# The tail of a Perceiver block on one core: a new order for the last tiles of the second output projection, a new Sinkhorn schedule with its scratch in PSUM, and VectorE mixing 24 units

## The chip, the cores and the metric

One core of a Trainium2 chip. The metric is the device time of one execution in microseconds. Before the change it is 1153.63 us, the median of three runs (1153.41 to 1156.05).

## The reference, cut to what matters

Three sublayers, each added to x, which has 8 x 64 tokens of 1024 numbers in float32: a cross attention with 32 heads, a self attention with 32 heads (its output projection is the last large product of the kernel), and a mixing block. Only the end of the second and the third matter here:

```python
x = x + attention2(layernorm(x))                 # ... @ Wo.T, with causal mask
# third sublayer, on h = layernorm(x) of this x:
x_norm = h * rsqrt(mean(h * h) + eps)
L      = x_norm @ [W_res; W_pre; W_post].T + base          # 16 + 4 + 4 numbers a token
H_res  = sinkhorn_log(L[16] as 4x4, 50 iterations, tau 0.1) # rows and columns in turn
H_pre, H_post = softmax(L[4]), softmax(L[4])
H_res  = (1 - g) * I + g * H_res                             # g = sigmoid(gate)
y      = (sum_n H_pre[n] * h[n]) @ W_branch                  # h as 4 streams of 256
out    = x + (H_res @ h_streams + H_post x y)
```

A Sinkhorn iteration here works on K = exp(logits / tau), shifted: it makes the row sums of K * v, inverts them to u, makes the column sums of K * u, inverts them to v.

## The kernel before, in words

The kernel is written by hand in five programs, one for each engine, tied by semaphores; nothing is reordered by a planner, so the order of the text is the order of the work. Tokens are four tiles (t = 0 to 3) of 128 rows. PSUM has eight banks of 512 numbers (`ps[:, k, :]`). Weights are transposed by VectorE (L1373), and split in a high part (ScalarE, L967) and a low part (VectorE, L1381); a tile of 512 output columns takes 24 matmuls (L864): eight chunks of the contraction, three products each.

**The last products.** The loop `for b in range(16)` (L885, TensorE) does the second attention's query units 21 and 22 (b = 0 to 7) and its output projection as units 23 (columns 0 to 511, b = 8 to 11, tiles 0 to 3) and 24 (columns 512 to 1023, b = 12 to 15, tiles 0 to 3). The attention itself is woven in up to b = 10: transposed queries (L733), scores (L750), transposed probabilities (L765), weighing (L780), transposed outputs (L790). On VectorE the loop L1789 serves the same steps: in step b it adds the product of step b - 1 to x (`add_tile`, L1663) with half of its statistics (L1784), reads scores (L1730), scales outputs (L1744, L1750), centres (L1736, L1738), transposes weight chunks (`turns`), makes their low parts (`later`: of unit 24 chunks 0, 1 in step 9, 2 to 4 in step 10, 5 to 7 in step 11) and the low part of an output (L1759), on which the second half of the next L765 waits.

When the second half of a tile's row is added (`last_stats3`, L1812), VectorE ends its statistics and GpSimd takes two roots (L2036). TensorE transposes the finished rows (`turn_rows`, L801), ScalarE copies them out (L1259), TensorE makes the 24 logits (`logits`, L810, 16 records a tile), and VectorE reads them (L1830, L1833). W_branch and the three small matrices arrive by DMA (L443, L445) and are transposed at L917; L923 multiplies them by a matrix of ones.

**The Sinkhorn chains.** The four tiles are two chains of VectorE instructions: chain 0 for tiles 0 and 1, chain 1 for tiles 2 and 3. An iteration is six small instructions, each waiting for the one before it in its chain:

```python
            def iterate(chains, fresh=None, last=None):        # L1916
                ... tk = Kx * v        (L1921)   ... ua = row sums of tk   (L1927)
                ... ua = 1 / ua        (L1930)   ... tk = Kx * ua          (L1903)
                ... v  = column sums   (L1906)   ... v  = 1 / v            (L1910)
```

With both chains given, the instructions of the two alternate. All operands lie in the SBUF tile `small`. Chain 0 does its first iteration and HEAD = 4 more alone (L1977 to L1980), then the logits of tile 3 are read (L1981), chain 1 is set up and does its first iteration, and 20 iterations are done jointly. Then the epoch: each chain's sums go through a logarithm on ScalarE (`log_chain`), are added to the logits (`recentre`, L1940) and exponentiated anew, while the other chain does 4 iterations alone; then 21 joint iterations, `finish(0)` (L1951 to L1956), 4 iterations of chain 1 alone and `finish(1)`. From the start of chain 1's first iteration to the end of its last that is 20 + 4 + 4 + 21 + 4 = 53 turns. VectorE's queue is in order, so nothing of it overlaps anything else of VectorE.

**Branch and mixing.** ScalarE and TensorE make the branch y of each tile (L1289, L822, L829) and its base x + H_post * y (L839, L843); tiles 0 and 1 stay open in banks (0, 1) and (2, 3), tiles 2 and 3 go through banks (4, 5) back to SBUF (L1302). The final mixing has 64 units of 128x256 (tile, output stream i, input stream j). For tiles 0 and 1 ScalarE makes 32 diagonal matrices when chain 0 is finished (L1336), TensorE multiplies (L853, two records a product) and ScalarE copies out (L1341). For tiles 2 and 3 VectorE does 32 instructions after chain 1 (L2023): tile 2 with all four streams at once, tile 3 in two halves. SyncE stores in five DMAs (L446 to L450), in the order tile 0, tile 2, tile 1, tile 3 first half, tile 3 second half, each waiting for its part.

Of the kernel before, what the change touches and what calls it, by code (L numbers as in the profile page):

```python
# [25 lines left out]
P = 128  # L26
# [11 lines left out]
ITERS, EPOCH, HEAD = 50, 25, 4  # L38
# [10 lines left out]
def perceiver(nc, x, ctx_in, mask_x, wq1, wk1, wv1, wo1, qn_w, kn_w, wq2, wk2, wv2, wo2,  # L49
# [10 lines left out]
    with es:  # L60
# [76 lines left out]
        tk = cols(64)  # L137
        uv = cols(32)
        luv = cols(32)
# [154 lines left out]
        def _(sp):  # L294
# [156 lines left out]
            sp.wait_ge(out_stored, 16 * 5)  # L451
# [3 lines left out]
        def _(pe):  # L455
# [337 lines left out]
            def turn_rows(t, half):  # L793

                pe.wait_ge(acc_free, (57 if half else 53) + t)
                if t == 0:
                    pe.wait_ge(o2_lo, 8)
                else:
                    pe.wait_ge(f_ready, 2 * t - 1 + half)
# [5 lines left out]
            def logits(t):  # L805
                pe.wait_ge(f_ready, 2 * t + 2)
                if t >= 2:
                    pe.wait_ge(lg_read, t - 1)
                for c in range(NC):
                    mm = pe.matmul(lg[t % 2], xT[t % 2][:, c, :], w24T[:, c, :], start=(c == 0), stop=(c == NC - 1))  # L810
                mm.then_inc(lg_done, 1)
# [20 lines left out]
            def base(t):  # L832

                pe.wait_ge(lg_read, 4)
                if t == 3:
                    pe.wait_ge(base_added, 1)
                for half in range(2):
                    bank = ps[:, base_banks[t][half], :]
# [3 lines left out]
                    for i in (2 * half, 2 * half + 1):  # L842
                        mm = pe.matmul(bank[:, (i % 2) * CW:(i % 2 + 1) * CW], dmix[t % 2][:, 4 + i, :], yb,  # L843
                                       start=False, stop=(t >= 2 and i % 2 == 1))
                mm.then_inc(base_done, 1)

            def mix(t):
                for half in range(2):
                    bank = ps[:, base_banks[t][half], :]
                    for i in (2 * half, 2 * half + 1):  # L850
                        for j in range(NSTR):
                            pe.wait_ge(d_res, 16 * t + 4 * i + j + 1)
                            mm = pe.matmul(bank[:, (i % 2) * CW:(i % 2 + 1) * CW], dres[t][:, 4 * i + j, :],  # L853
# [31 lines left out]
            for b in range(16):  # L885
                n, t = 21 + b // NT, b % NT
                pe.wait_ge(acc_free, 43 + b)
# [3 lines left out]
                def at_11():  # L891
                    if b == 0:
                        turn_key(2)
                    elif b <= 8:
                        turn_query(b - 1)
                    elif b >= 12:
                        if b >= 13:
                            turn_rows(b - 13, 1)
                        turn_rows(b - 12, 0)

                def at_17():
                    if 3 <= b <= 10:
                        turn_out2(b - 3)
                tile_products(n, t, at_11, at_17)
# [8 lines left out]
                if b == 11:  # L913
# [5 lines left out]
                if b == 12:  # L919
# [5 lines left out]
                if b >= 13:  # L925
                    logits(b - 13)
            turn_rows(3, 1)
            logits(3)
# [3 lines left out]
            for t in range(2):  # L932
                mix(t)
# [24 lines left out]
        def _(sc):  # L958
# [296 lines left out]
            def copy_rows(t, half):  # L1255
                sc.wait_ge(f_done, 2 * t + half + 1)
# [10 lines left out]
            asked = [0, 0]  # L1267

            def answer(c, dst, src, func):

                asked[c] += 1
                sc.wait_ge(sk_in[c], asked[c])
                sc.activation(dst, src, func).then_inc(sk_out[c], 1)
# [4 lines left out]
            def log_chain(c):  # L1278
                answer(c, luv.rearrange("p (s c n) -> p c s n", s=2, c=2)[:, c],
                       uv.rearrange("p (s c n) -> p c s n", s=2, c=2)[:, c], ACT.Ln)  # L1280

            def branch(t):
# [16 lines left out]
                if t >= 2:  # L1299
                    sc.wait_ge(base_done, t + 1)  # L1300
                    for half in range(2):
                        a = sc.activation(xr[:, t, half * UW:(half + 1) * UW], ps[:, base_banks[t][half], :], ACT.Copy)  # L1302
                    a.then_inc(base_added, 1)

            copy_rows(0, 0)
            sc.wait_ge(s24_done, 1)
            sc.activation(s24, ps[:, 3, 192:216], ACT.Copy).then_inc(s24_ready, 1)
            copy_rows(0, 1)
            copy_rows(1, 0)
            normalise_out(0)  # L1310
            copy_rows(1, 1)
            copy_rows(2, 0)
            normalise_out(1)
            copy_rows(2, 1)
            copy_rows(3, 0)
            exp_chain(0)
            exp_chain(0)
            copy_rows(3, 1)
            normalise_out(2)
            exp_chain(1)  # L1320
# [4 lines left out]
            branch(0)  # L1325
            branch(1)
            log_chain(0)
            exp_chain(0)
            log_chain(1)
            exp_chain(1)  # L1330
            branch(2)
            branch(3)
            for t in range(2):
                sc.wait_ge(h_ready, 1)
                for n in range(16):
                    sc.activation(dres[t][:, n, :], ident[:], ACT.Copy, scale=hres[:, 16 * t + n:16 * t + n + 1]  # L1336
# [805 lines left out]
```

## Time and profile before

| what | value |
|---|---|
| median of 3 runs | 1153.63 us |
| the profiled execution, its own time | 1153.41 us |
| its span, first to last instruction | 1151.6 us |
| TensorE matmul busy | 1071.5 us (93%) |
| VectorE busy | 808.7 us (70%) |
| ScalarE busy | 477.0 us (41%) |
| granted TensorE clock over the span | 0.978 |

Busy shares are means over the whole span. Starts in the trace's views are microseconds from the span's start. In a timeline a row is one or more instructions of one line in a row: start, time from the first's start to the last's end, engine, line, operation, operands and count; in brackets the idle time before it and what ended it.

### The profile page before, as it was taken

The page shows a single profiled execution, that of the slowest core. Times are in us where ns is not written, and L with a number is a line of the kernel's source. Part 1 is how long each engine was busy: PE and PEld are TensorE (multiplying, and loading weights), DVE is VectorE, ACT ScalarE, POOL GpSimd, SP SyncE. Part 2 cuts the span into 40 slices and gives each one's busy share as a digit, 9 for nine tenths or more (in the row PEclk, how much of TensorE's full clock was granted, in tenths as well). Part 3 has the DMA queues.
Part 4 walks back from the last instruction along what each step waited for, and adds up shares of the span by engine and source line. Part 5 has one row for each costly group of instructions (what it writes and reads, how often), then busy time and mean ns, then how long its engine had stood idle before and what let it go on. Part 6 is the DMA issues. An engine that isn't in the chain of part 4 may idle for free.

```text
span 1151.6 us, 17668 instructions
## 1 busy us (share of the span) xinstructions
PE 1071.5 (93%) x6392; PEld 899.6 (78%) x6392; DVE 808.7 (70%) x1843; ACT 477.0 (41%) x989; POOL 154.7 (13%) x162
## 2 busy tenths in 40 slices
PE   5999999999999999999999999999999999895565
PEld 3888888888888887888888887888888778784444
DVE  6744447567768868776678876675547799836998
ACT  4523324354454446544544455432223334313334
POOL 0000000333223222332332220000001000000000
PEclk9999999999999999999999999999999999997778
DMA  9876757243443233344334312899835322000001
GB/s 236 189 163 144 159 124 168 55 101 89 102 105 73 68 73 69 75 98 101 93 90 104 70 33 61 172 218 245 172 74 109 57 42 35 14 2 1 0 1 73
DMA packets 163803, 111.12 MB, mean 96 GB/s; under 512 B 73224, under 2 KB 155784, under 8 KB 163744
## 3 DMA queue, kind: packets, MB, share of 16 engines
q1 hardware_dynamic: 161488, 109.24, 43.3%
q10 hardware_dynamic: 2256, 1.11, 0.4%
q8 instruction: 35, 0.57, 0.2%
q14 instruction: 24, 0.20, 0.1%
HBM read 90.91 MB, written 18.87 MB: 95 GB/s over the span
## 4 chain that ended last, share of the span: by engine, by line
PE 82%; DVE 14%; ACT 2%; issue 1%; DMA 1%; POOL 0%; ACTq 0%; DVEq 0%
PE ps L533 29%; PE ps L476 28%; PE ps L864 8%; PE ps L462 5%; PE ps L544 4%; PE ps L561 4%; DVE wt L1381 1%; DVE xr L2023 1%; DVE small L1906 1%; DVE small L1930 1%; DVE small L1910 1%; DVE small L1903 1%; DVE small L1927 1%; DVE small L1921 1%; PE ps L650 1%
## 5 line engine op out<-in xcount | busy, mean ns | idle before, releaser
L533 PE MATMUL ps<-wt,act 128*128 128x512 f32 x1536 | 389.1, 396 | 0.0
L476 PE MATMUL ps<-wt,act 128*128 128x512 f32 x1440 | 330.1, 391 | 4.0 <-DVE wt L1381 3.9
L476 PEld LDWEIGHTS ps<-wt,act 128*128 128x128 f32 x1440 | 271.1, 189 | 60.8 <-DVE act L1365 4.3
L533 PEld LDWEIGHTS ps<-wt,act 128*128 128x128 f32 x1536 | 275.9, 188 | 49.5
L1381 DVE TENSOR_TENSOR wt<-raw,wt 128x512 fp32r<-128x512 f32 x192 | 120.0, 682 | 84.9 <-ACT wt L967 84.9
L967 ACT ACTIVATE wt<-raw 128x512 fp32r<-128x512 f32 x192 | 106.5, 623 | 94.5 <-PE ps L476 52.7
L1365 DVE TENSOR_TENSOR act<-ps,act 128x512 fp32r<-128x512 f32 x112 | 75.9, 683 | 78.4 <-ACT act L962 78.4
L1373 DVE STREAM_TRANSPOSE raw<-raw 128x1024 f32<-128x1024 f32 x92 | 108.0, 1217 | 31.4 <-DMA raw<-in_L_xattn_o_proj_w 20.7
L864 PE MATMUL ps<-wt,act 128*128 128x512 f32 x480 | 121.0, 400 | 1.7 <-issue 1.0
L962 ACT ACTIVATE act<-ps 128x512 fp32r<-128x512 f32 x112 | 65.9, 596 | 114.2 <-PE ps L462 113.9
L2036 POOL TENSOR_TENSOR small<-small 128x4 f32<-128x4 f32 (+2 forms) x64 | 70.8, 1109 | 278.5 <-DVE small L1395 213.7
L864 PEld LDWEIGHTS ps<-wt,act 128*128 128x128 f32 x480 | 87.0, 188 | 19.8 <-issue 1.7
L1047 ACT ACTIVATE G<-G,small 128x256 f32<-128x256 f32 x128 | 64.1, 502 | 80.7 <-DVE small L1492 80.7
L2063 POOL TENSOR_TENSOR act<-xr,act 128x1024 fp32r<-128x1024 f32 x30 | 71.9, 2396 | 110.2 <-ACT act L1000 110.2
L462 PE MATMUL ps<-ident,G 128*128 128x128 f32 x448 | 67.4, 276 | 16.2 <-ACT G L973 10.3
L462 PEld LDWEIGHTS ps<-ident,G 128*128 128x128 f32 x448 | 54.5, 141 | 30.6 <-issue 9.9
L544 PE MATMUL ps<-act 128*128 128x256 f32 x384 | 60.0, 292 | 0.6 <-DVE act L1365 0.6
L1012 ACT ACTIVATE G<-ps 128x512 f32<-128x512 f32 x32 | 19.1, 598 | 97.3 <-PE ps L476 97.3
L1488 DVE SCALAR_TENSOR_TENSOR G<-ps,small,G 128x256 f32<-128x256 f32 x128 | 55.4, 474 | 5.7 <-PE ps L544 5.7
L561 PEld LDWEIGHTS ps<-act 128*128 128x128 f32 x384 | 54.4, 189 | 5.5 <-DVE act L1365 0.4
L2054 POOL TENSOR_TENSOR small<-small 128x4 f32<-128x4 f32 x32 | 6.5, 202 | 374.6 <-DVE small L1509 374.6
L561 PE MATMUL ps<-act 128*128 128x256 f32 x384 | 56.2, 282 | 0.0
(145 smaller groups left out, 1086.4 us busy)
## 6 DMA issues: line engine op xcount, KB each, us to landing
xr<-in_ctx SPq DMA_DIRECT2D x64, 256.0 KB, 5.7
raw<-in_L_xattn_o_proj_w SPq DMA_DIRECT2D x32, 512.0 KB, 13.9
raw<-in_L_xattn_q_proj_w SPq DMA_DIRECT2D x28, 512.0 KB, 9.6
q_rows<-G SPq DMA_DIRECT2D x64, 128.0 KB, 3.5
xr<-q_rows SPq DMA_DIRECT2D x16, 512.0 KB
ot_hi<-spare SPq DMA_DIRECT2D x64, 128.0 KB, 2.6
act<-ot_hi SPq DMA_DIRECT2D x32, 256.0 KB, 9.0
raw<-in_L_xattn_k_proj_w SPq DMA_DIRECT2D x8, 512.0 KB, 9.0
```

What stands on the lines that cost most here:

```text
L462: tr = pe.transpose(bank[par][:, j * P:(j + 1) * P], src, ident[:])
L476: mm = pe.matmul(banks[t], lhs(p == 2, c, t), wt[:, n_slot, int(p == 1), c, :], start=(acc_from and q == 0), stop=(acc_to and q == 3 * NC ...
L533: mm = pe.matmul(bank, src[int(p == 2)][:, c, kt * P:(kt + 1) * P], wt[:, slot, int(p == 1), c, :], start=(q == 0), stop=(q == 3 * NC - 1))
L544: mm = pe.matmul(sacc[:, j * 256:(j + 1) * 256], lhs[p], kT[r][:, g, :], start=(p == 0 and r == 0), stop=(p == 1))
L561: mm = pe.matmul(oacc, vN[r][:, kt, g * P:(g + 1) * P], pT[p][:, kt * 256:(kt + 1) * 256], start=(n == 0), stop=(n == 5))
L864: mm = pe.matmul(acc2[t], act[:, int(n >= 23), int(p == 2), k:k + P], wt[:, n % 2, int(p == 1), c, :], start=(q == 0), stop=(q == 3 * NC - 1))
L967: sc.activation(blocks16(wt_dst(par, 0, c)), raw_chunks(par, c) if slot is None else raw_chunks(slot, c), ACT.Copy).then_inc(w_hi, 1)
L1365: v.tensor_tensor(dst, four(bank[par]) if shaped else bank[par], hi_.bitcast(F32), ALU.subtract).then_inc(lo_done, 1)
L1373: v.transpose(y, y).then_inc(w_turned, 1)
L1381: v.tensor_tensor(blocks16(wt_dst(par, 1, c)), raw_chunks(slot, c), blocks16(wt_dst(par, 0, c)).bitcast(F32), ALU.subtract).then_inc(w_lo, 1)
L2036: pool.tensor_tensor(dst, src, mhalf[:, 0:n], ALU.pow).then_inc(signals, 1)
L2063: pool.tensor_tensor(ctx_dst(ctxT, 1, kt), ctx_src(kt), ctx_dst(ctxT, 0, kt).bitcast(F32), ALU.subtract).then_inc(ctx_lo, 1)
```

## The change

1. Order of the output projection: a hand-written order of tile and half replaces "all first halves, then all second halves". Steps b = 8 to 15 now do (tile, half) = (0,0), (1,0), (0,1), (1,1), (2,0), (3,0), (2,1), (3,1). Unit 24 is thus first used in step 10 in place of step 12, so its low parts are made in steps 9 (chunks 0 to 3) and 10 (chunks 4 to 7). The half statistics of tiles 0 and 1 move behind the low part of step 10.
2. The transposes of rows and the logits follow the new order; the logits of tile 2 and the first half of those of tile 3 are computed inside step 15, ahead of its last six matmuls.
3. Chain 0 starts after the logits of tile 1 and does 1 + 3 + 3 + 1 iterations (`LEAD`) between the last additions. The reading of tile 3's logits comes after the last of these.
4. The epoch needs no logarithm: ScalarE gives exp of half the centred logits once (`answer(c, A, 0.5)`), and in iteration 25 the scaled matrix becomes the new Kx by `fold_outer` (in place of the column scaling) and two multiplications by that root (`fold_root`, twice). Chains stay joint through it. After chain 1's first iteration there are 41 joint ones, one with the finish of chain 0 woven in, and 7 of chain 1 alone: 49 turns.
5. `tk` (scaled matrix) and the row sums `us` are in PSUM bank 5; `Kx` and the column sums `vs` stay in SBUF.
6. Mixing: the first half of tile 2 goes to TensorE (bank 4, 8 more diagonals and 8 more products, after those of tile 1), the rest of tiles 2 and 3 stays with VectorE as 16 + 8 instructions. Bases that go back to SBUF use the upper halves of banks 6 and 7. There are six stores, the first half of tile 2 third in order.

```diff
-ITERS, EPOCH, HEAD = 50, 25, 4
+ITERS, EPOCH = 50, 25
+LEAD = (1, 3, 3, 1)
+LAST = ((0, 0), (1, 0), (0, 1), (1, 1), (2, 0), (3, 0), (2, 1), (3, 1))
...
+        tk, us = ps[:, 5, 0:64], ps[:, 5, 64:80]
...
-        base_banks = [(0, 1), (2, 3), (4, 5), (4, 5)]
+        open_banks = [(ps[:, 0, :], ps[:, 1, :]), (ps[:, 2, :], ps[:, 3, :]), (ps[:, 4, :],)]
+        late_base = ps[:, 6:8, 256:512]
...
-            for t, half, signal, count in ((0, None, mix_out, 2), (2, None, out_ready, 1), (1, None, mix_out, 4),
-                                           (3, 0, out_ready, 2), (3, 1, out_ready, 3)):
+            for t, half, signal, count in ((0, None, mix_out, 2), (1, None, mix_out, 4), (2, 0, mix_out, 5),
+                                           (2, 1, out_ready, 1), (3, 0, out_ready, 2), (3, 1, out_ready, 3)):
...
             for b in range(16):
                 n, t = 21 + b // NT, b % NT
+                if b >= 8:
+                    t, n = LAST[b - 8][0], 23 + LAST[b - 8][1]
...
-                    elif b >= 12:
-                        if b >= 13:
-                            turn_rows(b - 13, 1)
-                        turn_rows(b - 12, 0)
+                    elif b == 11:
+                        turn_rows(0, 0)
+                        turn_rows(0, 1)
+                    elif b == 12:
+                        logits(0)
+                        turn_rows(1, 0)
+                        turn_rows(1, 1)
+                    elif b == 13:
+                        turn_rows(2, 0)
+                    elif b == 14:
+                        turn_rows(3, 0)
+                    elif b == 15:
+                        turn_rows(2, 1)
...
+                    if b == 15:
+                        logits(2)
+                        logits(3, 0, 4)
...
             turn_rows(3, 1)
-            logits(3)
+            logits(3, 4, NC)
             for t in range(NT):
                 branch(t)
                 base(t)
-            for t in range(2):
+            for t in range(3):
                 mix(t)
...
-                     6: (23, (4, 5)), 7: (23, (6, 7)), 9: (24, (0, 1)), 10: (24, (2, 3, 4)), 11: (24, (5, 6, 7))}
+                     6: (23, (4, 5)), 7: (23, (6, 7)), 9: (24, (0, 1, 2, 3)), 10: (24, (4, 5, 6, 7))}
...
             def exp_chain(c):
-                answer(c, Kx[:, 32 * c:32 * c + 32], A[:, 32 * c:32 * c + 32], ACT.Exp)
+                sc.wait_ge(sk_in[c], 1)
+                answer(c, Kx)
+                sc.wait_ge(sk_in[c], 2)
+                answer(c, Kx)
+                sc.wait_ge(sk_out[c], 2)
+                answer(c, A, 0.5)
...
+            diagonals(0)
+            diagonals(1)
+            mixed(0, 0)
+            mixed(0, 1)
+            mixed(1, 0)
+            diagonals(2)
+            mixed(1, 1)
+            mixed(2, 0)
...
-            ua = [uv[:, 8 * c:8 * c + 8] for c in range(2)]
-            ub = [uv[:, 16 + 8 * c:24 + 8 * c] for c in range(2)]
+            ua = [us[:, 8 * c:8 * c + 8] for c in range(2)]
+            ub = [vs[:, 8 * c:8 * c + 8] for c in range(2)]
...
+            def iterate(chains):
+
+                fold = [c for c in chains if iterated[c] == EPOCH]
                 for c in chains:
+                    iterated[c] += 1
+                    if c in fold:
+                        fold_outer(c)
+                    else:
+                        scale_cols(c)
+                for c in fold:
+                    fold_root(c, tk)
+                    fold_root(c, Kx)
...
-            last_stats3(0)
-            last_stats3(1)
+            add_last(1, 1)
             logits(0)
-            last_stats3(2)
+            add_last(2, 0)
             logits(1)
             centre_rows(0)
             centre_cols(0)
-            last_stats3(3)
             first_iteration3(0)
+            for _ in range(LEAD[0]):
+                iterate((0,))
+            add_last(3, 0)
+            for _ in range(LEAD[1]):
+                iterate((0,))
+            add_last(2, 1)
+            for _ in range(LEAD[2]):
+                iterate((0,))
             logits(2)
-            for _ in range(HEAD):
+            add_last(3, 1)
+            for _ in range(LEAD[3]):
                 iterate((0,))
             logits(3)
             centre_rows(1)
+            centre_cols(1)
...
             first_iteration3(1)
-            joint = EPOCH - 1 - HEAD
-            for k in range(joint):
-                iterate((0, 1), last=0 if k == joint - 1 else None)
+            for k in range(ITERS - iterated[0]):
+                iterate((0, 1))
...
+            v.wait_ge(base_added, 3)
+            mix(((2, 1), (3, 0)))
+            mix(((3, 1),))
```

## Rows read from the trace of the kernel before

**Rows 1.** The chain that ended last, its shares of the span by engine.
```profile
PE 82%; DVE 14%; ACT 2%; issue 1%; DMA 1%; POOL 0%; ACTq 0%; DVEq 0%
```
**Rows 2.** Busy time by stretch: length, PE, PEld, DVE, ACT, POOL, clock, DMA share, GB/s.
```profile
1062.50:1098.70 36.20, 15.29 (x64) 11.78 (x64) 34.59 (x268) 14.66 (x36) 0.00 (x0) 0.69 0.00 1
...
1128.60:1134.90 6.30, 5.75 (x20) 4.88 (x21) 5.37 (x29) 6.21 (x22) 0.00 (x0) 0.72 0.00 0
1134.90:1145.40 10.50, 9.79 (x46) 8.28 (x44) 10.15 (x24) 5.40 (x16) 0.00 (x0) 1.00 0.25 100
```
**Rows 3.** Timeline of VectorE between the last product and chain 1's first iteration.
```profile
1047.92 0.69 DVE L1663 TENSOR_TENSOR xr<-ps,xr 128x512 f32<-128x512 f32 x1 [1.28 <-PE ps L864]
...
1049.81 0.18 DVE L1903 TENSOR_TENSOR small<-small 128x32 f32<-128x32 f32 x1
...
1056.21 0.20 DVE L1830 SCALAR_TENSOR_TENSOR G<-G,small,ps 128x24 f32<-128x24 f32 x1
...
1058.76 0.19 DVE L1903 TENSOR_TENSOR small<-small 128x32 f32<-128x32 f32 x1 [0.30 <-ACT small L1273]
```
**Rows 4.** Timeline of VectorE, first instruction of successive iterations: joint, then alone.
```profile
1069.57 0.31 DVE L1921 TENSOR_TENSOR small<-small 128x32 f32<-128x32 f32 x2
...
1070.96 0.30 DVE L1921 TENSOR_TENSOR small<-small 128x32 f32<-128x32 f32 x2
...
1131.34 0.19 DVE L1921 TENSOR_TENSOR small<-small 128x32 f32<-128x32 f32 x1
...
1132.73 0.19 DVE L1921 TENSOR_TENSOR small<-small 128x32 f32<-128x32 f32 x1
```
**Rows 5.** Matmul records of the logits of one tile, in the chain.
```profile
1039.70 1.70 PE ps L810 x16
```
**Rows 6.** Timeline around steps 9 and 10 of the loop, VectorE and TensorE.
```profile
1001.38 0.68 DVE L1759 TENSOR_TENSOR act<-ps,act 128x512 fp32r<-128x512 f32 x1
...
1002.12 0.65 PE L765 MATMUL ps<-ident,raw 128*128 128x128 f32 x4 [1.21 <-DVE act L1759]
...
1004.53 4.40 PE L864 MATMUL ps<-wt,act 128*128 128x512 f32 x18
...
1005.70 1.89 DVE L1381 TENSOR_TENSOR wt<-raw,wt 128x512 fp32r<-128x512 f32 x3
```
**Rows 7.** Timeline of the mixing on ScalarE and TensorE.
```profile
1128.69 9.45 ACT L1336 ACTIVATE raw<-ident,small 128x128 f32<-128x128 f32 x32 [7.04 <-DVE small L1956]
...
1129.15 15.55 PE L853 MATMUL ps<-G,raw 128*128 128x256 f32 x64 [8.61 <-ACT raw L1336]
```
**Rows 8.** The chain's mixing on VectorE, in order of time, and the last stores.
```profile
1134.89 1.69 DVE xr L2023 x4
...
1141.82 0.89 DVE xr L2023 x2
...
1145.56 0.89 DVE xr L2023 x2
...
out<-xr SPq DMA_DIRECT2D x2, 256.0 KB, 2.5
```
**Rows 9.** VectorE's groups by form (busy us, mean ns), without and with a PSUM operand.
```profile
L1921 DVE TENSOR_TENSOR small<-small 128x32 f32<-128x32 f32 x96 | 15.4, 191 | 0.4
...
L1930 DVE RECIPROCAL small<-small 128x8 f32<-128x8 f32 x98 | 16.3, 200 | 0.6
...
L1744 DVE RECIPROCAL small<-ps 128x16 f32<-128x16 f32 x8 | 2.0, 249 | 3.1 <-PE ps L780 3.1
...
L1833 DVE SCALAR_TENSOR_TENSOR small<-G,small 128x24 f32<-128x24 f32 x4 | 1.0, 244 | 0.1
L1830 DVE SCALAR_TENSOR_TENSOR G<-G,small,ps 128x24 f32<-128x24 f32 x4 | 0.9, 213 | 0.0
```
**Rows 10.** Timeline of VectorE: two independent instructions that read PSUM, one behind the other.
```profile
889.90 0.28 DVE L1699 TENSOR_TENSOR spare<-ps,G 128x128 f32<-128x128 f32 x1
890.10 0.28 DVE L1700 TENSOR_TENSOR spare<-ps,G 128x128 f32<-128x128 f32 x1
```

More of the change, by code:

```diff
@@ L803, in turn_rows, with logits @@
                 tr.then_inc(f_done, 1)
-            def logits(t):
-                pe.wait_ge(f_ready, 2 * t + 2)
-                if t >= 2:
+            def logits(t, c0=0, c1=NC):
+                pe.wait_ge(f_ready, max(TURNED[t, h][0] for h in range(c0 // 4, (c1 + 3) // 4)))
+                if c0 == 0 and t >= 2:
                     pe.wait_ge(lg_read, t - 1)
-                for c in range(NC):
+                for c in range(c0, c1):
                     mm = pe.matmul(lg[t % 2], xT[t % 2][:, c, :], w24T[:, c, :], start=(c == 0), stop=(c == NC - 1))
-                mm.then_inc(lg_done, 1)
+                if c1 == NC:
+                    mm.then_inc(lg_done, 1)
             def branch(t):
@@ L834, in base @@
                 pe.wait_ge(lg_read, 4)
[L835 to L838, printed above, removed]
+                for half in range((2, 2, 1, 0)[t]):
+                    bank = open_banks[t][half]
                     pe.matmul(bank, ident[:], xr[:, t, half * UW:(half + 1) * UW], start=True, stop=False)
@@ L1255, in copy_rows @@
             def copy_rows(t, half):
-                sc.wait_ge(f_done, 2 * t + half + 1)
+                sc.wait_ge(f_done, TURNED[t, half][0])
                 if half == 0 and t >= 2:
@@ new lines, in invert_rows, with scale_rows, sum_cols, invert_cols @@
+            def invert_rows(c):
+                stepped(c)
+                step(c, v.reciprocal(ua[c], ua[c]))
+            def scale_rows(c):
+                stepped(c)
+                step(c, v.tensor_tensor(rows3(of(tk, c)), rows3(of(Kx, c)), over_j(ua[c]), ALU.mult))
+            def sum_cols(c):
+                stepped(c)
+                step(c, v.tensor_reduce(two(ub[c]), cols4(of(tk, c)), AX, ALU.add))
+            def invert_cols(c):
+                stepped(c)
+                step(c, v.reciprocal(ub[c], ub[c]))
@@ new lines, in first_iteration3, with fold_outer, fold_root @@
+            def first_iteration3(c):
+                answered(c, 2)
+                scale_rows(c)
+                sum_cols(c)
+                invert_cols(c)
+            def fold_outer(c):
+                stepped(c)
+                rows = two(ua[c]).unsqueeze(3).broadcast_to([P, 2, NSTR, NSTR])
+                step(c, v.tensor_tensor(rows4(of(tk, c)), rows, over_i(ub[c]), ALU.mult))
+            def fold_root(c, dst):
+                answered(c, 3)
+                stepped(c)
+                step(c, v.tensor_tensor(of(dst, c), of(tk, c), of(A, c), ALU.mult))
@@ L1999, in _, with mix @@
                     done(v.tensor_tensor(h8r, h8r, h8m.unsqueeze(2).broadcast_to([P, 8, NSTR]), ALU.mult), mix_ready)
-            for k in range(HEAD):
-                if k == HEAD // 2:
-                    recentre(0)
-                iterate((1,), last=1 if k == HEAD - 1 else None)
-            for k in range(HEAD):
-                if k == HEAD // 2:
-                    recentre(1)
-                iterate((0,), fresh=0 if k == 0 else None)
-            for k in range(ITERS - EPOCH - HEAD):
-                iterate((0, 1), fresh=1 if k == 0 else None)
-            finish(0)
-            for k in range(HEAD):
+            iterated[1] += 1
+            finish_cols(0)
+            scale_cols(1)
+            finish_gate(0)
+            sum_rows(1, tk)
+            finish_diagonal(0)
+            invert_rows(1)
+            scale_rows(1)
+            sum_cols(1)
+            invert_cols(1)
+            for _ in range(ITERS - iterated[1]):
                 iterate((1,))
-            finish(1)
+            finish_cols(1)
+            finish_gate(1)
+            finish_diagonal(1)
             settle()
-            for t, parts in ((2, ((0, 1, 2, 3),)), (3, ((0, 1), (2, 3)))):
-                v.wait_ge(base_added, t - 1)
-                for streams in parts:
-                    for j in range(NSTR):
-                        settle()
-                        for i in streams:
+            def mix(pieces):
+                for j in range(NSTR):
+                    settle()
+                    for t, half in pieces:
+                        for i in (2 * half, 2 * half + 1):
                             c = 16 * t + 4 * i + j
```

231 lines of the change are left out of this document (107 added, 124 removed).

## The prediction

> **What bounds the kernel now.** I read the chain that ended last first. TensorE has 82% of it and VectorE 14% [rows 1]: products carry the kernel until the last tile at 1047.92 us [rows 3], and from there VectorE carries nearly all of the last 104 us. The table by stretch confirms it: from 1062.5 to 1098.7 VectorE is busy 34.59 of 36.20 us, TensorE 15.29, ScalarE 14.66 [rows 2]. So a saving outside VectorE's queue in the tail is worth nothing, and one inside it is worth its full length unless ScalarE, TensorE or the stores end later.
>
> In the tail there are four pieces: from the last product to chain 1's first iteration (1047.92 to 1058.76, rows 3), 53 turns of the chains, the finish, and VectorE's mixing from 1134.89 [rows 8]. A joint iteration takes 1.39 us (1069.57 to 1070.96) and one of a chain alone takes the same 1.39 (1131.34 to 1132.73) [rows 4]. That is six steps of 0.232 us: the length is the wait of an instruction for its predecessor, and the second chain rides for nothing. It rides nearly at the limit, though. Two instructions of L1921 together last 0.31, one lasts 0.19 [rows 4, 9], so the second starts 0.12 after the first, half a step. Shorter waits can help a joint turn only a little, unless an instruction also occupies the engine for less.
>
> **The change, part by part.** Times are against the profiled execution (span 1151.6, own time 1153.41, 0.2 under the median).
>
> *Unit 24 two steps earlier.* Step 9 now makes four low parts in place of two, ahead of L1759, and the second half of L765 waits for that (it was idle 1.21 us for it already) [rows 6]. Three low parts last 1.89 us, so two are 1.25 us: TensorE is later by +1.2. The statistics that leave step 9 (0.7) don't pay for it, as VectorE then waits for the products of L780 anyway. In step 10 the product starts at 1004.53 + 1.2 = 1005.8 and wants chunk 4 after 12 matmuls at 0.24 us (18 last 4.40), 1008.7; VectorE makes it from about 1006.9, after scaling the outputs, to 1007.6, and chunk 7 to 1009.5 against 1010.7 or later. Covered, by about 1 us at the tightest. The small matrices' transposes move to the end of step 10, about 1012; their DMAs are issued once the last weighing is done, 1005.9, and a store of the largest one's 256 KB takes 2.5 us [rows 8], so they are there by 1010.
>
> *Logits inside step 15.* One tile's logits and half of another's come ahead of the last matmuls: 1.70 + 0.85 = +2.55 us [rows 5]. The transposes move but stay the same number before the last product's end (8 halves less one). So the last product ends at 1047.9 + 1.2 + 2.55 = 1051.7.
>
> *Chain 0's lead.* Its 1 + 3 + 3 iterations (9.7 us) must fit between additions. Chain 0 is set up after step 12, which I place at 1031; its first iteration and one more end at about 1035.6, the product of step 13 at 1037.4. A further three take 4.2 us of the 6.2 us of step 14 (5.5 us of products and 0.6 of transposes), beside 1.4 of addition and statistics; the same again in step 15 with 1.9. They fit by 0.5 us in step 14 and more in step 15, so they cost nothing. If they did not fit, TensorE's next transpose would wait for the addition queued behind them, at most 1.4 us.
>
> *Chain 1's start.* Behind the last product stand the addition and last statistics, 1.89 us (1047.92 to 1049.81), one iteration, 1.39, then the logits: 1051.7 + 3.3 = 1055.0 in place of 1056.21 [rows 3]. TensorE's last transposes, the copy and half of the logits need about 3.2 us in the same time, a near tie. From there to the first iteration is the same work, 2.55 us. Gain: -1.2.
>
> *The turns.* 49 in place of 53: 4 x 1.39 = -5.6. Two recentrings at 0.2 go (-0.4), the steps that a fresh matrix spared come back (+0.2), the finish of chain 0, 0.6 us alone, is woven into a turn (-0.6). The two folds add two dependent steps each: 4 x 0.232 = +0.9, and here the other chain waits. Together -5.4; I take -5.2, since the woven finish has some longer instructions. The logarithms go from ScalarE, which was not on the path.
>
> *Mixing.* Half a tile leaves VectorE. A half lasts 1145.56 - 1141.82 = 3.7 us [rows 8]; the remaining 16 go four to a step as tile 2 did (6.9 us for 16) and the last 8 as a half. -3.7.
>
> *The other side of the mixing.* Let T be the finish of chain 0. ScalarE's 32 diagonals take 9.45 and TensorE's 32 products 15.6 us from 0.45 after it [rows 7], to T + 16.1. The eight further diagonals can start after the third copy, T + 13.4, and are done at T + 15.8; eight products at 0.43 (46 records in the 9.8 to 10.1 us after 1134.9 [rows 2]) end at T + 19.5, their copy at T + 20.2. VectorE: T + 11.4 (0.9 for the rest of the woven turn, 7 x 1.39, finish 0.75) + 6.9 + 3.7 = T + 22.0. TensorE's side has 1.8 us to spare. But SyncE waits in order, so three stores of 256 KB start at T + 20.2 to 21 and share the engines with the last, where before the last had them alone (2.5 us [rows 8]): +0.5.
>
> *PSUM.* The operands of five of six steps change: four write PSUM, four read it. No VectorE instruction before writes PSUM. Reads: 24 columns take 213 ns with a PSUM operand and 244 without [rows 9]; 128 columns take 281 ns with PSUM [rows 10] against 191 for 32 without [rows 9], 0.94 ns for each further column, so nothing is left for PSUM; the reciprocal of 16 numbers from PSUM takes 249, that of 8 from SBUF 200, a difference that the numbers or the memory may make. Occupancy: two independent PSUM readers of 128 columns start 0.20 apart [rows 10]; without 128 x 0.94 ns that leaves 0.08, and a chain's pair leaves 0.12 - 0.03 = 0.09. So reading PSUM is as quick as SBUF or some 10 ns quicker. Bounds for a touched instruction: -31 ns (244 to 213) and +49 (the reciprocals, all of it put on PSUM); for the writes I keep the same two, having nothing nearer. I take -10 ns for each of the four reading steps and nothing for the writes: 0.04 a turn, x 49 = 2.0, of which the occupancy limit may keep back some: -1.7.
>
> The Trainium skill says the opposite ("VectorE: DVE Perf Modes", section "The TRN2 errata"): a fixed 58 cycles at 0.96 GHz for SBUF sources and 120 for PSUM sources, an estimated 65 ns more per instruction. By it the sum would end near 1167, above the time before. For reads the rows here disagree with it; for writes no row shows either.
>
> Sum: -1.2 - 5.2 - 3.7 + 0.5 - 1.7 = -11.3; 1153.4 - 11.3 = 1142.1 us.
>
> **The rivals.**
> *A, PSUM is dearer (slower).* If each touched instruction occupies VectorE for d more, a joint turn pays eight of them, since the engine is nearly full, and a turn alone four: 41 x 8 + 8 x 4 = 360 d, against the 9.6 us gained without PSUM. Break-even is d = 27 ns; at the upper bound, 49 ns, it is +17.6, 1161 us; at 10 to 20 ns, 1147 to 1151. Against it stand the reads [rows 9, 10]; for it, that no write was seen and that the two reciprocals differ. Chance 0.15: 0.04 still faster, 0.04 level, 0.07 slower. The skill's page of above is a rule for this side.
> *B, the lead stalls TensorE.* Unit 24 or the lead comes late in steps 10 to 15 by 2 to 4 us: 1145 to 1148, faster all the same. Room of 0.9 and 0.5 us speaks both ways. Chance 0.08.
> *C, TensorE's mixing becomes the end.* The granted clock was 0.72 as the mixing began after a gap and 1.00 later [rows 2]; branches now end earlier, so the gap is longer. If the first half of the 40 products went at 1.2 GHz, some 0.4 us more each, that is +8 less the spare 1.8: about 1148. Before, it rose after some 3 us. Chance 0.05.
> *D, PSUM is quicker than I take.* Occupancy falls by 12 ns per touched instruction: 360 x 0.012 = 4.3, 1139.5; at twice that 1135. Chance 0.2.
> *E, the chains don't gain,* because a joint turn of one fold blocks both and the order of semaphores costs what the four turns gave: 1148 to 1152. The steps are all in the trace already, so 0.02.
>
> **How the numbers follow.** Forecast 1142.1, between 1139.5 and 1146, has 0.5. The range is 1135 to 1150: it takes in B, C, D and the cheap end of A. What the measurement can tell from no change is 0.3%, 3.5 us. Faster by more (under 1150.2): 0.5 + D 0.2 + B 0.08 + C 0.05 + A 0.04 = 0.87; same: A 0.04 + E 0.02 = 0.06; slower: A 0.07.
>
> **What would show it.** In the new trace: the last product's addition at 1051 to 1052; chain 1's first iteration near 1057.5; a joint turn of 1.33 to 1.39 us (above 1.45 is A, under 1.30 is D); 24 mixing instructions in 10.6 us; the last copy on ScalarE 1 to 2 us ahead of VectorE's end. It is wrong if a turn departs by over 0.1 us, or if the last addition is past 1054.

## The result and the profile after

The median of four runs is 1146.84 us (1146.20 to 1147.55), against 1154.84 us (1153.41 to 1156.87) for four runs of the kernel before on the same chip: ratio 0.9934, interval 0.9919 to 0.9948, so faster. The profiled execution took 1146.2 us with a span of 1144.4 (before 1153.41 and 1151.6): the span is 7.2 us shorter, where the working asked for 11.3; by the medians it is 8.0. Direction and range held, but about a third of the expected gain is missing, and the time lies just above the 1139.5 to 1146 us to which the forecast gave even chances.

The chain that ended last, shares of the span by engine [answers to rows 1]:

```profile
PE 81%; DVE 14%; DMA 2%; ACT 2%; issue 1%; ACTq 0%; POOL 0%; DVEq 0%; SPq 0%
```

The shares hardly moved, so they can't say where the gain went. VectorE's timeline can (start, time, engine, line, operation, operands, count, idle time before and what ended it) [rows 3, 4, 8]:

```profile
1044.02 0.69 DVE L1700 TENSOR_TENSOR xr<-ps,xr 128x512 f32<-128x512 f32 x1 [0.41 <-PE ps L884]
...
1052.66 0.69 DVE L1700 TENSOR_TENSOR xr<-ps,xr 128x512 f32<-128x512 f32 x1 [1.86 <-PE ps L884]
...
1058.13 0.19 DVE L1954 TENSOR_TENSOR ps<-small,ps 128x32 f32<-128x32 f32 x1
...
1058.71 0.32 DVE L1942 TENSOR_TENSOR ps<-small 128x32 f32<-128x32 f32 x2
...
1060.12 0.32 DVE L1942 TENSOR_TENSOR ps<-small 128x32 f32<-128x32 f32 x2
...
1130.57 10.53 DVE L2092 SCALAR_TENSOR_TENSOR xr<-G,small,xr 128x256 f32<-128x256 f32 x24
```

Cut at the same milestones, the two spans differ so:

| from, to | before | after | difference | forecast |
|---|---|---|---|---|
| start, last addition | 1047.92 | 1052.66 | | |
| start, chain 1's first iteration | 1058.76 | 1058.13 | -0.6 | -1.2 |
| to VectorE's mixing (the turns) | 76.13 | 72.43 | -3.7 | -6.9 (turns -5.2, PSUM -1.7) |
| VectorE's mixing | 14.30 | 10.53 | -3.8 | -3.7 |
| to the end of the span | 2.41 | 3.30 | +0.9 | +0.5 |

Four turns went, yet a joint turn lasts 1.41 us (1058.71 to 1060.12) where it took 1.39 [rows 4]. By form, between 1060 and 1120 us (busy us, mean ns of one) [rows 9]:

```profile
L1950 DVE RECIPROCAL ps<-ps 128x8 f32<-128x8 f32 x81 | 13.4, 210 | 0.0
L1962 DVE RECIPROCAL small<-small 128x8 f32<-128x8 f32 x83 | 13.0, 196 | 0.0
L1942 DVE TENSOR_TENSOR ps<-small 128x32 f32<-128x32 f32 x80 | 12.6, 198 | 0.0
L1954 DVE TENSOR_TENSOR ps<-small,ps 128x32 f32<-128x32 f32 x81 | 12.5, 194 | 0.0
L1946 DVE TENSOR_REDUCE ps<-ps 128x8 f32<-128x32 f32 x79 | 12.5, 198 | 0.0
L1958 DVE TENSOR_REDUCE small<-ps 128x8 f32<-128x32 f32 x81 | 12.3, 189 | 0.0
```

The reciprocal that reads and writes PSUM takes 210 ns where the one in SBUF [rows 9] takes 200. TensorE around steps 9 and 10 [rows 6], and the busy time by stretch (columns of rows 2):

```profile
1001.43 0.60 PE L769 MATMUL ps<-ident,raw 128*128 128x128 f32 x4
1002.96 0.66 PE L769 MATMUL ps<-ident,raw 128*128 128x128 f32 x4 [0.93 <-DVE act L1796]
1004.30 1.74 PE L784 MATMUL ps<-G,raw 64*64 64x33 f32 x64 [0.69 <-ACT raw L1255]
1005.97 5.32 PE L884 MATMUL ps<-wt,act 128*128 128x512 f32 x18
```

```profile
1004.00:1012.00 8.00, 7.70 (x88) 6.57 (x89) 3.42 (x7) 2.57 (x6) 0.00 (x0) 0.79 0.18 48
```

The 18 matmuls that lasted 4.40 us [rows 6] last 5.32, and the granted clock of the stretch is 0.79 where it had been 1.00: part of it ran at 1.2 GHz in place of 2.4.

### The profile page after: what moved, and what is told of

Its sections match the earlier page's. It is cut to its first block, busy times and chain, and to the rows that moved or that the text cites. A ratio compares the mean times of both kernels' runs of the same rounds, so it can differ in the third digit from the quotient of the medians.

```text
span 1144.4 us, 17715 instructions
## 1 busy us (share of the span) xinstructions
PE 1076.0 (94%) x6414; PEld 903.8 (79%) x6414; DVE 807.2 (71%) x1837; ACT 475.1 (42%) x991; POOL 155.6 (14%) x162
## 4 chain that ended last, share of the span: by engine, by line
PE 81%; DVE 14%; DMA 2%; ACT 2%; issue 1%; ACTq 0%; POOL 0%; DVEq 0%; SPq 0%
PE ps L480 28%; PE ps L537 27%; PE ps L884 8%; PE ps L466 5%; PE ps L548 3%; PE ps L565 3%; DVE wt L1418 2%; DMA xr<-q_rows 1%; DVE ps L1950 1%; DVE small L1962 1%; DVE ps L1954 1%; DVE ps L1946 1%; DVE small L1958 1%; DVE ps L1942 1%; PE ps L654 1%
```

## The experiments

Four questions: what PSUM does to a turn, what the wait in step 9 does to TensorE, what the order of the stores costs, and what chain 0's lead buys. Every experiment is the changed kernel with the edit shown. They ran on three chips: each ratio is against the kernel before on the same chip, and medians of different chips are compared only roughly.

**All scratch in SBUF.**

```diff
-        vs = cols(16)
-        tk, us = ps[:, 5, 0:64], ps[:, 5, 64:80]
+        vs, us, tk = cols(16), cols(16), cols(64)
```

> The changed kernel with the scaled matrix and the row sums in SBUF again, as before; all else as changed. Theory P (the PSUM operands make a turn longer): a turn goes from 1.41 us to the 1.39 of before, alone and joint; over 49 turns the mixing on VectorE starts 1.1 to 1.3 us earlier after chain 1's first iteration (71.2 us in place of 72.4), and the span ends near 1143.2. Theory Q (the longer turn comes from TensorE and ScalarE being busier beside the chains, or from the new order of instructions): a turn stays at 1.41 and the span at 1144.4. The forecast's own view (PSUM quicker by 10 ns a reading step): a turn gets longer, 1.45.

Ratio 0.9932 (0.9919 to 0.9944), median 1145.41 us, by time no different from the change. Its groups by form in the same stretch:

```profile
L1961 DVE RECIPROCAL small<-small 128x8 f32<-128x8 f32 x83 | 13.3, 201 | 0.0
L1957 DVE TENSOR_REDUCE small<-small 128x8 f32<-128x32 f32 x83 | 13.3, 200 | 0.0
L1949 DVE RECIPROCAL small<-small 128x8 f32<-128x8 f32 x83 | 13.2, 200 | 0.0
L1953 DVE TENSOR_TENSOR small<-small 128x32 f32<-128x32 f32 x83 | 12.7, 191 | 0.0
L1941 DVE TENSOR_TENSOR small<-small 128x32 f32<-128x32 f32 x81 | 12.6, 191 | 0.0
L1945 DVE TENSOR_REDUCE small<-small 128x8 f32<-128x32 f32 x83 | 12.5, 186 | 0.0
```

The turns go back to 1.39 us and their stretch to 71.28 (1059.56 to 1130.84), 1.15 shorter: that is PSUM's share. TensorE at work beside the chains is not what makes PSUM dear: from 1100.7 to 1118 us, where it is idle in the changed kernel, the reciprocal on PSUM takes 217 ns and the other five forms 190 to 200, against 207 and 188 to 198 while it works (1064 to 1100). The span did not shrink, since in this execution the clock between 1004 and 1012 was 0.57 and the last addition came at 1054.12, 1.5 later. A single profiled span doesn't show one microsecond of the chains; their own stretch does, and it is what I compare below. It repeats well: 72.43 to 72.45 us in all seven executions with the change's scratch.

**One operand at a time.** Only the matrix `tk`, only the sums `us`, or only the matrix scaled by rows, in a buffer of its own:

```diff
# matrix only
-        vs = cols(16)
-        tk, us = ps[:, 5, 0:64], ps[:, 5, 64:80]
+        vs, us = cols(16), cols(16)
+        tk = ps[:, 5, 0:64]
# sums only
+        vs, tk = cols(16), cols(64)
+        us = ps[:, 5, 64:80]
# rows-scaled matrix only; tr is also what sum_cols and finish_cols read
+        vs, us, tk = cols(16), cols(16), cols(64)
+        tr = ps[:, 5, 0:64]
-step(c, v.tensor_tensor(rows3(of(tk, c)), rows3(of(Kx, c)), over_j(ua[c]), ALU.mult))
+step(c, v.tensor_tensor(rows3(of(tr, c)), rows3(of(Kx, c)), over_j(ua[c]), ALU.mult))
```

> Only the scaled matrix in PSUM, the row sums in SBUF. Theory P, by the durations in the changed kernel against before (write of 32 numbers 201 against 193 ns, sum over columns read with a stride 191 against 202, reciprocal of the row sums 216 against 203): the reciprocal is back at 203, the sum over columns stays at 191, so a turn is 1.39 to 1.40. Theory Q: 1.41 as in the changed kernel.

> Only the row sums in PSUM, the scaled matrix in SBUF. Theory P: the reciprocal stays at 216 ns, the strided sum goes back to 202, the write of the matrix to 193: a turn of 1.41 to 1.42, the longest of the four. Theory Q: 1.41, the same as all the others.

> Only the matrix scaled by rows goes to PSUM, a buffer of its own, and is read from there by the strided sum over columns; the matrix scaled by columns, both kinds of sums and Kx are in SBUF. Theory P: the write costs 8 ns more and the strided read 11 less, so a turn is 1.385 to 1.39, not above the turn with all in SBUF. Theory Q: no difference among e1 to e4.

Each ran once: 1145.86, 1145.99 and 1144.93 us, too close to tell apart; the stretch of the turns tells them apart:

| scratch in PSUM | stretch of the turns | against all SBUF, per turn (of 49) |
|---|---|---|
| none | 71.28 | |
| matrix | 71.67 | +8 ns |
| sums | 71.95 | +14 ns |
| both (the change) | 72.43 | +23 ns |
| rows-scaled matrix alone | 71.01 | -6 ns |

The matrix alone, by form (1060 to 1120 us):

```profile
L1958 DVE TENSOR_REDUCE small<-ps 128x8 f32<-128x32 f32 x82 | 12.6, 190 | 0.1
L1946 DVE TENSOR_REDUCE small<-ps 128x8 f32<-128x32 f32 x80 | 12.3, 190 | 0.0
```

The upper line is the column sum, which reads across the rows of the matrix (200 with all in SBUF), the lower the row sum, which reads along them (186). The sums alone:

```profile
L1950 DVE RECIPROCAL ps<-ps 128x8 f32<-128x8 f32 x82 | 13.7, 212 | 0.0
L1946 DVE TENSOR_REDUCE ps<-small 128x8 f32<-128x32 f32 x82 | 12.7, 194 | 0.1
L1954 DVE TENSOR_TENSOR small<-small,ps 128x32 f32<-128x32 f32 x81 | 12.3, 186 | 0.0
```

So each use has its own price: writing PSUM costs 5 to 8 ns, the reciprocal on it 12, reading the matrix along its rows 4; the column sum gains 10 (190 against 200) and the multiplication by the inverted sums 5. The differences of the five forms with a PSUM operand add up to nearly what the turn does, since a step waits for the one before it: for the change +7 +12 +10 +3 -11 = +21 ns by form, +23 measured. The sixth form, the reciprocal in SBUF, was touched by no edit and still lies between 196 and 201 ns, so single differences of 5 ns and less are not sure. The version that keeps only the paying read in PSUM is the shortest of the five, by 0.27 us; two later kernels with this scratch show 71.02. The sums alone were expected to give the longest turn (1.41 to 1.42 us); it is the change itself that does.

**The wait in step 9.** The low part of the output, on which TensorE waits, goes ahead of the four low parts of unit 24:

```diff
+                if b == 9:
+                    lo_out2(b - 3)
                 if b in later:
                     for c in later[b][1]:
                         lo_unit(later[b][0], c)
-                if 3 <= b <= 10:
+                if 3 <= b <= 10 and b != 9:
                     lo_out2(b - 3)
```

> The changed kernel, but in step 9 VectorE makes the low part of the attention output (L1796) before the four low parts of unit 24, not behind them. Theory S (the four low parts ahead of it hold TensorE up, and the gap also lowers TensorE's granted clock in step 10, where the first 18 matmuls lasted 5.3 us against 4.4 before): the second half of the transposed probabilities starts near 1000.7 in place of 1003.0, the clock is 1.00 from 1004 to 1012, the last addition starts near 1049.5 in place of 1052.7, and the span is 1141 to 1142. Rival L (the last addition is late by the logits inside step 15 alone, and the clock dip is chance): the clock stays at 0.8 there, the last addition moves to 1051.5 at most and the span to 1143.

Ratio 0.9929 (0.9915 to 0.9943), median 1146.39 us: no more than the change, where a span of 1141 to 1142 us was expected. The wait is gone and the clock in step 10 is whole, but a stretch at 1.2 GHz came later. Its TensorE timeline:

```profile
1001.93 1.04 PE L769 MATMUL ps<-ident,raw 128*128 128x128 f32 x8
...
1004.77 4.38 PE L884 MATMUL ps<-wt,act 128*128 128x512 f32 x18
...
1046.24 2.75 PE L815 MATMUL ps<-G,raw 128*128 128x24 f32 x24
1048.84 2.53 PE L884 MATMUL ps<-wt,act 128*128 128x512 f32 x6
1052.15 1.12 PE L806 MATMUL ps<-ident,xr 128*128 128x128 f32 x4 [0.78 <-DVE xr L1700]
1053.95 1.90 PE L815 MATMUL ps<-G,raw 128*128 128x24 f32 x8 [0.69 <-ACT raw L1293]
```

The addition of step 14 comes 2.1 us earlier than in the changed kernel (1041.89 against 1044.02), but the last six matmuls take 2.53 us in place of 1.65, the last transposes 1.12 in place of 0.66 and the last logits 1.90 in place of 1.07. Chain 1's first iteration starts at 1058.17, where it was. The low clock was hardly chance of this one execution: the granted clock over the span was 0.976 to 0.979 in the five executions of this experiment, and 0.979 to 0.982 in the nine of the changed kernel.

**The order of the stores.** SyncE takes the late half of tile 2 and the first of tile 3, which VectorE finishes, ahead of the half that TensorE finishes:

```diff
-            for t, half, signal, count in ((0, None, mix_out, 2), (1, None, mix_out, 4), (2, 0, mix_out, 5),
-                                           (2, 1, out_ready, 1), (3, 0, out_ready, 2), (3, 1, out_ready, 3)):
+            for t, half, signal, count in ((0, None, mix_out, 2), (1, None, mix_out, 4), (2, 1, out_ready, 1),
+                                           (3, 0, out_ready, 2), (2, 0, mix_out, 5), (3, 1, out_ready, 3)):
```

> The changed kernel, but SyncE stores the second half of tile 2 and the first half of tile 3 before the first half of tile 2, which comes from TensorE. Theory T (the end hangs on TensorE's mixing through SyncE's order: three stores are issued only when ScalarE's last copy is done at 1139.9, and the last store 0.2 us late behind them): the two stores go out at 1137.5, the stretch from the end of VectorE's mixing to the end of the span goes from 3.3 to 2.5 us, the span to 1143.6. Rival: the last store takes its time anyway and the stretch stays at 3.0 or more.

Ratio 0.9917 (0.9901 to 0.9932), median 1145.12 us. From VectorE's end to the end of the span it is 2.45 us in place of 3.30. By the medians the gain over the change is 1.7 us, and the intervals overlap, so the time alone doesn't show it; the profiled span (1144.6) hides it, its last addition being at 1053.69. One profile would be thin, as this tail varies: in the nine executions with the old order and the full lead it is 2.87 to 4.05 us, 3.48 in the mean, and in the three with the new one 2.45 to 2.48.

**The first logits of tile 3 behind the last product.**

```diff
                     if b == 15:
                         logits(2)
-                        logits(3, 0, 4)
...
+            logits(3, 0, 4)
             turn_rows(3, 1)
             logits(3, 4, NC)
```

> The changed kernel, but the first half of the logits of tile 3 stands behind the last product of step 15, not ahead of its last six matmuls. By the trace the last product ends 0.85 us earlier and TensorE does the half while VectorE adds, so the last logits and chain 1's first iteration come 0.7 to 0.9 us earlier (1057.3 in place of 1058.1 at an equal start of step 15) and the span is 1143.6. If chain 1's start hangs on VectorE's queue (addition, statistics, one iteration) and not on TensorE, the gain is as large, since that queue starts with the last product too. Rival: the transposes of the last half wait behind the half of the logits and nothing is gained.

Ratio 0.9922 (0.9907 to 0.9937), median 1145.58 us. From the addition of step 14 to the last it is 7.74 us (1045.42 to 1053.16) in place of 8.64, and from there to chain 1's first iteration still 5.48: the eight records fit beside VectorE's last addition and cost nothing there. The wait of step 9 (2.51) and the low clock after it are as they were.

**Both of TensorE's edits together, and the change run again beside it.** The first joins the edits of step 9 and of the logits; the second is the changed kernel, unedited.

> The changed kernel with two edits together: the low part of the output first in step 9 (as e5) and the first half of tile 3's logits behind the last product (as e7). Theory C (each gap or thin stretch of TensorE is paid again in granted clock; e5 removed the one in step 10, but 24 thin matmul records in a row ahead of the last six products brought 1.2 GHz from 1049.3, e7 removed those but kept step 10's): with both gone the clock is 1.00 from 1004 to the last product, the last addition starts near 1048.5, 4 us before that of the changed kernel, and the time is 4 us under e10's. Rival A (the edits simply add): e5 and e7 gained 0 to 1 us each against the changed kernel, so 1 us or less under e10, and e8's gain came from the stores and the PSUM part.

> The changed kernel itself, unedited, on the same chip as its variants: 0.993 of the kernel before, 1144 to 1146 us beside 1153.5. Its last addition lies between 1052 and 1054 by how long TensorE runs at 1.2 GHz in steps 9 and 10. If that were chance of one execution, some profile would show 1051 as the sum of the forecast had it.

Ratios 0.9894 (0.9879 to 0.9910) and 0.9943 (0.9930 to 0.9957), medians 1141.08 and 1147.33: 6.2 us between them (5.6 by the ratios), where 4 were expected, and the intervals lie clear of each other. Each edit alone had stood 0.9 and 1.8 us under the change run again by the medians, on another chip, and 1.6 and 2.4 by the ratios, with intervals of some 1.7 us to either side that overlap that of the change. So the times show what the two give together, and not that it is more than their sum. TensorE's timeline of the changed kernel in this execution:

```profile
999.13 0.60 PE L769 MATMUL ps<-ident,raw 128*128 128x128 f32 x4
1002.24 0.66 PE L769 MATMUL ps<-ident,raw 128*128 128x128 f32 x4 [2.50 <-DVE act L1796]
1003.58 1.93 PE L784 MATMUL ps<-G,raw 64*64 64x33 f32 x64 [0.69 <-ACT raw L1255]
1005.44 6.36 PE L884 MATMUL ps<-wt,act 128*128 128x512 f32 x18
```

and of the joined edits:

```profile
999.21 1.35 PE L769 MATMUL ps<-ident,raw 128*128 128x128 f32 x8
1001.25 1.14 PE L784 MATMUL ps<-G,raw 64*64 64x33 f32 x64 [0.69 <-ACT raw L1255]
1002.31 4.40 PE L884 MATMUL ps<-wt,act 128*128 128x512 f32 x18
...
1043.80 1.86 PE L815 MATMUL ps<-G,raw 128*128 128x24 f32 x16
1045.50 1.65 PE L884 MATMUL ps<-wt,act 128*128 128x512 f32 x6
1046.99 0.97 PE L815 MATMUL ps<-G,raw 128*128 128x24 f32 x8
```

Both start level (999.1 and 999.2). The product of step 10 starts 3.1 us earlier without the wait: 2.5 for the wait and 0.8 for the weighing (1.14 against 1.93), less small things. It then lasts 1.96 us less. The logits give 0.9 more. That is 6.0, and the last addition is indeed at 1047.19 against 1053.17. So of the 5.1 us between the two up to the product's end nearly 2.8 (0.8 + 1.96) is granted clock that came after the wait. This is one pair of executions; the product alone varied by over 1 us where the wait stood (below).

**Everything that paid.** The rows-scaled matrix in PSUM, both of TensorE's edits and the order of the stores; and the same with the change's scratch.

> All together: low part of the output first in step 9, store order, half of the logits behind the product, and in the chains only the matrix scaled by rows in PSUM. If the parts add: 3.2 us from step 9, 0.8 from the logits, 0.8 from the stores and 1.4 from the turns, of which TensorE's mixing (its copy at 1139.9 in the changed kernel, VectorE's end at 1141.1) may keep back 0.5: a span near 1138.5, 0.5% under the changed kernel. If TensorE's mixing sets the end, the turns' part is lost and it is 1139.5 to 1140.

> e8 with the chains' scratch back in PSUM as the change has it (scaled matrix and row sums). Theory P: a turn is 1.416 us against 1.386 in e8, so the mixing on VectorE starts 1.4 us later, and since TensorE's side ends 1 us ahead in e8 all of it shows: 1139.5 to 1140.2 against 1138.6. Rival: TensorE's side sets the end in both (it too starts when chain 0 ends, after 41 joint turns, 1.2 us later) and the difference is the same 1.2, or nothing of it shows.

The first has ratio 0.9861 (0.9845 to 0.9876), median 1138.59 us, the shortest of all: 8.3 us under the change and 16 under the kernel before. The second, on another chip, has 0.9891 (0.9876 to 0.9907), median 1140.49. The stretch of the turns is 71.02 against 72.44, the same 1.4 us as between the two scratches without the other edits; the medians differ by 1.9 and the ratios by 3.5 us, with intervals that touch.

**A shorter lead.** The joined version with `LEAD = (1, 1, 1, 1)` in place of `(1, 3, 3, 1)`.

> e8 with LEAD = (1, 1, 1, 1): chain 0 does 4 iterations ahead of chain 1 in place of 8, then 45 joint turns and 3 of chain 1 alone. Chain 1 still has 49 turns, so VectorE's mixing starts when it did (1124.6); but chain 0 ends 4 turns later (1113.3 + 5.6 = 1118.9), and TensorE's mixing, 20.2 us from there to its record's end and 0.6 of copy, ends at 1139.7, past VectorE's 1135.1. Theory T (the lead buys TensorE's side its time and not the chains): the span is 1142 to 1142.5, 4.5 us more. Rival (the lead buys turns): VectorE's mixing itself starts 5.6 us later, at 1130.2.

Ratio 0.9914 (0.9899 to 0.9929), median 1144.16 us, 5.6 above the joined version, though VectorE's mixing starts no later (1124.15 against 1124.60). The chain that ended last, from 1128 us on:

```profile
1127.92 11.24 PE ps L873 x52
1139.16 0.02 issue
1139.18 0.60 ACT xr L1370
```

VectorE is done at 1134.68; the end is TensorE's mixing, which waits for chain 0's finish. The lead doesn't shorten the turns, since chain 1 sets their number. It gives TensorE its time.

## Why the prediction was right, and where it was off

**Right.** *Mixing:* -3.8 for -3.7. *Chain 0's lead:* forecast to fit by 0.5 us in step 14, it fits by 0.41, the idle time before the addition at 1044.02. *The turns without PSUM:* the stretch with all scratch in SBUF is 76.13 - 71.28 = 4.85 us shorter, for 5.2. *The wait of step 9:* forecast 1.21 + 1.25 = 2.46; the changed kernel showed 2.50 in its second profile, and 2.48 to 2.51 in the six experiments that leave step 9 as it is.

**Failed: the PSUM term.** "I take -10 ns for each of the four reading steps and nothing for the writes", -1.7 in the sum; measured +1.15, a miss of 2.9 and the largest. The reads were judged by other forms: a multiply-add of 24 columns and the reciprocals [rows 9]. The multiply-add's row does not even hold for itself. In the changed kernel the same instruction, which reads the same bank, is 4 ns quicker than its neighbour in SBUF, and not 31 (by form, 1020 to 1060 us):

```profile
L1878 DVE SCALAR_TENSOR_TENSOR small<-G,small 128x24 f32<-128x24 f32 x4 | 1.0, 244 | 0.1
L1875 DVE SCALAR_TENSOR_TENSOR G<-G,small,ps 128x24 f32<-128x24 f32 x4 | 1.0, 240 | 4.7 <-PE ps L815 4.7
```

The 213 ns of before were a mean of four that lay between 197 and 229; what made them short is not shown. The reciprocal's row (249 with PSUM, 200 without) was the nearest to a step of the chain, and it pointed the other way; with PSUM the chain's own reciprocal takes 10 to 12 ns more, a quarter of that difference. And the sign of the writes was left at nothing. Rival A's formula was off as well: it let a joint turn pay for both chains, eight times d, but joint and alone it lasts 1.41 us (the last turns alone: 1124.13 to 1125.54). It pays once. Rival A had the direction, at +23 ns a turn; D, a PSUM quicker still, is refuted.

The rule that was weighed there ("VectorE: DVE Perf Modes" of the Trainium skill, section "The TRN2 errata", an estimated 65 ns more for a PSUM source) is not what these runs show either: the differences by form are -11 to +12 ns. Taken one operand at a time, two of the four reading steps are dearer (+4, +12) and two cheaper (-10, -5).

**Off in size: the start of chain 1.** Forecast -1.2, measured -0.6. The last addition was to come at 1051.7 and came at 1052.66; the product of step 10 starts 1.44 us later than before (forecast 1.2), and its 18 matmuls then take 0.92 us more, which the sum took at 0.24 us each, as in rows 6. Both parts hold low clock: in this execution the product of step 9 (18 records, 5.96 us in place of 4.38) and the weighing (1.74 for 1.14) ran in part at 1.2 GHz too, and the wait of step 9 was only 0.93 because TensorE itself was late. The prediction looked for a low clock in the mixing (rival C), behind the long gap, and took it as full everywhere else. From the last addition on it was 0.4 us better than forecast. The stall of rival B did not come: from the product of step 10 at 1005.97 us to its last product TensorE never waits.

**Off in size: the end.** +0.9 for +0.5. The three late stores were foreseen. TensorE's side had 1.2 us to spare in place of 1.8: its last copy ends at 1139.93, VectorE at 1141.10. Rival C shows there in small: behind a gap of 18.86 us (8.61 before, rows 7) the granted clock was 0.50 for 3 us as before, but then 0.78 for 3.5 more, and the last copy ended 20.9 us behind the finish of chain 0 and not 20.2. With the stores in order of readiness about 1 us comes back (3.48 to 2.46 in the means above).

Added up: 0.6 + 0.35 + 2.85 - 0.1 + 0.4 = 4.1, the difference between -11.3 and -7.2. The range held because the missed terms are small beside it, not because the PSUM term was right.

## What to carry to other kernels

In a chain of small dependent instructions a change in the duration of a step shows nearly in full, so a change of memory is worth what each form gains or loses, times the turns; try it operand by operand and compare the chain's own stretch, not the span. When an engine that carries the kernel is made to wait, count what its granted clock costs behind the wait too, and test edits against such waits together: here two that could hardly be told from no change alone gave six microseconds together. Where one chain feeds another engine, its lead buys that engine's time, even where it buys nothing on the engine that runs the chain; and stores that wait in order belong in the order in which their data is ready.

## What was not expected of the hardware

A low clock of TensorE followed the waits within a busy stretch, not only the long gap of the tail. In all eight executions whose step 9 makes TensorE wait ahead of its second transposes (0.93 or some 2.5 us), the weighing or product right behind it ran in part at 1.2 GHz, 5.3 to 6.7 us for the 18 records of the product; in all five without that wait these 18 took 4.38 to 4.40. The length of the wait alone doesn't decide it: the kernel before waited 1.21 us there without such a fall [rows 6], and the changed kernel's first execution had one behind 0.93. Two executions, the changed kernel's first and that of the low part first, had a further fall in the product of step 9 (5.96 and 5.97 us). TensorE had idled 1.35 and 1.65 us ahead of it, hardly longer than in executions where that product took 4.38 (1.35 and, in the kernel before, 1.64).

What stays open is the fall in step 15 of the experiment on step 9. It came behind 24 records of 24 columns in a row, and the four profiles with only 16 there and no wait in step 9 had none; but the changed kernel has the same 24 records, at 1048.38, and kept 2.4 GHz. So the runs show that the two edits together are 6 us better than the change, and not what lets the clock fall.

A small sum that reads PSUM across rows is quicker than from SBUF (190 against 200 ns), while one that reads along rows is slower (190 against 186). Both read 32 numbers and write 8; they differ in the direction of the read, and why that changes the sign is not shown.
